# The second group's convolution inside the first group's turn, and info and mask in strips of 32 partitions

## What is computed

```
# 1. gated convolution on the group-normalised x
info = relu(info_w @ gn(x) + info_b)                 # 16 channels
mask = sigmoid(mask_w @ gn(x) + mask_b)              # 16 channels
x = x + relu(out_w @ (mask outer info) + out_b)      # 256 products -> 64 channels
# 2. linear attention on tokens t (1024 per image, one sequence per image)
t = t + attention(layernorm(t))     # q, k, v, elu+1, KV, Z, Wm, LN, W1, relu, W2, LN
# 3. mixture of 8 experts, top 2
h = layernorm(t); probs = softmax(h @ gate_w + gate_b); keep the two largest
t = t + sum over experts of weight * (gelu(h @ W1[e] + b1[e]) @ W2[e] + b2[e])
```

## Time and profile before

| | us |
|---|---|
| median of three runs | 1230.57 (1230.32 to 1233.61) |
| profiled execution, whole | 1232.37 |
| its span, first to last instruction | 1230.6 |
| PE busy | 1067.6 (87%) |
| DVE busy | 849.7 (69%) |
| ACT busy | 696.5 (57%) |
| POOL busy | 362.3 (29%) |
| mean granted TensorE clock | 0.972 of full speed |

### The profile page before, as it was taken

How to read it: one execution, slowest core, us unless ns; L and a number is a source line. 1 busy time by engine, 2 the same in 40 slices (tenths; PEclk the granted TensorE clock), 3 DMA queues, 4 the chain that set the end, 5 groups by cost and what they waited for, 6 DMA issues and landing times.

```text
span 1230.6 us, 14702 instructions
## 1 busy us (share of the span) xinstructions
PE 1067.6 (87%) x5430; PEld 502.1 (41%) x5430; DVE 849.7 (69%) x1767; ACT 696.5 (57%) x960; POOL 362.3 (29%) x276
## 2 busy tenths in 40 slices
PE   4776598989999798997989989998989979899897
PEld 2454245433454245442454433642344424444232
DVE  5665768588676976588774886859765796657543
ACT  3424365665656646656457656466565565576454
POOL 0100022234312333134231343133431233323466
PEclk8878599999999999999999999999999999999999
DMA  3110194005910086100940049200671009310480
GB/s 109 35 35 1 24 214 109 1 18 116 214 35 18 1 185 144 35 19 21 224 115 4 18 90 213 62 1 18 142 187 35 18 3 216 78 35 18 102 199 29
DMA packets 16119, 96.56 MB, mean 78 GB/s; under 512 B 3056, under 2 KB 5424, under 8 KB 11824
## 3 DMA queue, kind: packets, MB, share of 16 engines
q1 hardware_dynamic: 16048, 95.62, 33.4%
HBM read 77.79 MB, written 9.44 MB: 71 GB/s over the span
## 4 chain that ended last, share of the span: by engine, by line
PE 53%; DVE 26%; ACT 16%; issue 3%; DMA 1%; POOL 0%; DVEq 0%; POOLq 0%; SPq 0%; ACTq 0%
PE HP L691 9%; PE HP L676 9%; PE R L538 8%; PE R L486 5%; PE R L493 4%; ACT H L818 4%; PE R L504 4%; DVE SM L992 3%; PE R L615 3%; DVE T L1019 3%; PE R L552 3%; PE R L622 2%; DVE TM L1147 2%; PE R L691 2%; DVE BIG L1055 2%
## 5 line engine op out<-in xcount | busy, mean ns | idle before, releaser
L858 POOL TENSOR_TENSOR XB<-TM,XB 128x512 f32<-128x512 f32 x256 | 324.8, 1290 | 804.5 <-DVE TM L1147 804.4
L818 ACT ACTIVATE H<-HP,W 128x1024 f32<-128x1024 f32 x224 | 237.7, 1115 | 111.3 <-PE HP L676 110.1
L676 PE MATMUL HP<-XF,W1E 64*128 64x512 f32 x1024 | 255.1, 616 | 24.9 <-DVE TM L1147 24.5
L691 PE MATMUL HP<-H,W 128*64 128x512 f32 x896 | 226.5, 614 | 25.7 <-ACT H L818 25.7
L1147 DVE SCALAR_TENSOR_TENSOR TM<-HP,B2S,CWB 128x512 f32<-128x512 f32 x224 | 158.7, 741 | 119.1 <-PE HP L691 116.6
L676 PEld LDWEIGHTS HP<-XF,W1E 64*128 64x128 f32 x1024 | 87.3, 185 | 143.3 <-DVE TM L1147 82.5
L754 ACT ACTIVATE T<-R 128x512 f32<-128x512 f32 x128 | 74.0, 599 | 93.3 <-PE R L538 81.3
L691 PEld LDWEIGHTS HP<-H,W 128*64 128x64 f32 x896 | 49.9, 135 | 171.6 <-ACT H L818 119.6
L992 DVE TENSOR_REDUCE SM<-T 128x8 f32<-128x512 f32 x128 | 85.7, 684 | 41.5 <-ACT T L754 40.9
L968 DVE SCALAR_TENSOR_TENSOR BIG<-R,T 128x512 f32<-128x512 f32 x128 | 79.4, 682 | 23.6 <-PE R L486 23.6
L504 PE MATMUL R<-W,T 128*128 128x128 f32 x512 | 74.9, 294 | 15.0 <-DVE T L1011 14.0
(11 more groups left out here) (120 smaller groups left out, 1403.5 us busy)
## 6 DMA issues: line engine op xcount, KB each, us to landing
CWB<-gates_hbm SPq DMA_DIRECT2D x32, 1536.0 KB, 21.3
CWB<-gates_hbm SPq DMA_DIRECT2D x32, 512.0 KB, 9.7
X<-x SPq DMA_DIRECT2D x16, 512.0 KB, 5.9
BIG<-XN SPq DMA_DIRECT2D x32, 256.0 KB, 4.5
out<-XB SPq DMA_DIRECT2D x16, 512.0 KB, 2.7
W<-wpack SPq DMA_DIRECT2D x1, 1176.0 KB, 7.0
gates_hbm<-CWR SPq DMA_DIRECT2D x16, 64.0 KB, 1.6
W1E<-w1e SPq DMA_DIRECT2D x1, 512.0 KB, 8.4
```

Source lines behind the costliest of these rows:

```text
L676: last = mm(HP[u % BATCH][:, half(k)], W1E[img(k), e, :], XF[img(k), 1 - par, s, half(c)], start=True, stop=True)
L691: last = mm(sums_of(b, u)[img(k), :], w("w2e")[:, C * e:C * e + C], activated(b, u)[:, k, :], start=True, stop=True)
L818: f(activated(b, u).rearrange("p k t -> p (k t)"), HP[u % BATCH][:, :], ACT.Gelu, bias=col(B1E + e))\
L858: nc.gpsimd.tensor_tensor(acc, TM[:, u % BATCH, :], acc, ALU.add).then_inc(acc_done, 1)
```

## The change

1. Group 1 (EARLY) has its convolution inside turn 0. A list OPENING replaces the table for that turn; entries with `next` are stages of group 1. Its buffers are ones that nothing uses then: XF[:, 1] for the input (loaded at the start), the planes 0 to 6 of CWB for XN, T1, T2 and BIG, and HP for R. In turn 1 the convolution's stages are left out, centre_1 waits for the router's use of the R banks (cwt_done), and the input of group 2 is loaded into X in turn 1.
2. Info and mask of a slot lie in strips of 32 partitions, for the two pieces of 512 columns: info of slot s in strips 2s and 2s+1, mask in the other two; IM holds the high part and the rest behind each other in the columns. info_mask is four matmuls of 32 columns of weights into one bank, one ACT operation for info and one for mask (64 partitions), one cast and one subtraction on DVE (128 partitions). A replication is two matmuls of 32 rows that add up, for each piece. REP is loaded as eight pieces, the biases as eight small strips (BI).
3. The small statistics of the group norm have a tile of their own (SG), KVM lies in T1, and the chain's semaphore counts are kept by a running count.
4. SCHEDULE has other places for H and Y (eight batches ahead of `first_unit`, eight behind), conv_out.1 ahead of conv_out.0, `first_unit` behind centre_1.1, and finish_0 ahead of rstd_4.

The pieces stand in the order of the file: the tables, the turn, the strips and buffers, then PE's info_mask, replicate and centre_1, ACT's info_mask, DVE's info_mask. Names with a small a behind them (Xa, Ra, BIGa) are what convolution_buffers returns.

```diff
 SCHEDULE = [
-    ("channel_stats", "H"), ("gates", ""), ("gate_tokens", "Y"), ("gate_exp", ""), ("group_stats", "H"),
+    ("channel_stats", "H"), ("gates", ""), ("gate_tokens", ""), ("gate_exp", "Y"), ("group_stats", ""),
...
+EARLY = 1
+OPENING = [
...
+    "low_1.1", "high_1.0", "high_1.1", "conv_out.0", "next group_stats", "conv_out.1", "centre_1.1",
...
+            if a == 0:
+                ahead, _ = parts(EARLY, None, 1 - par)
+                for name in OPENING:
+                    first, _, rest = name.partition(" ")
+                    stage = ahead.get(rest) if rest else stages.get(name)
+                    if stage:
+                        stage()
+                return
...
+        def strip(kind, s, c):
+
+            q = 2 * (s ^ kind) + c
+            return slice(32 * q, 32 * q + 32)
...
+        def convolution_buffers(a):
+
+            if a == EARLY:
+                return XF[:, 1, :, :], CWB[:, :, 0, :], CWB[:, :, 1, :], CWB[:, :, 2, :], CWB[:, :, 3:7, :], HP
+            return X, XN, T1, T2, BIG, R
...
-                    for c in range(NCH):
-                        mm(R[s][img(c), half(c)], w("wim"), XN[:, s, half(c)], start=True, stop=True)\
-                            .then_inc(im_ps, 1)
+                    for kind in range(2):
+                        for c in range(NCH):
+                            last = mm(Ra[s][strip(kind, s, c), 0:CH], w("wim")[:, 32 * kind:32 * kind + 32], XNa[:, s, half(c)],
+                                      start=True, stop=True)
+                    last.then_inc(im_ps, 1)
...
                 def replicate(n, slots):
 
                     if n == 0 and starting(a):
                         pe.wait_ge(prep_done, 1)
                         pe.wait_ge(act_prep, 2)
-                    for s, c in pieces(slots):
+                    for s in slots:
                         if n == 0:
-                            pe.wait_ge(hl_done, nth(a + 1, s, c))
-                            if exists(a - 1):
+                            pe.wait_ge(hl_done, nth(a + 1, s))
+                            if exists(a - 1) and a != EARLY:
                                 pe.wait_ge(cwt_done, a)
                         elif n % 3 == 1:
-                            pe.wait_ge(ir_done[s], at(a * 2 + n // 3 + 1, c))
+                            pe.wait_ge(ir_done[s], at(a * 2 + n // 3 + 1, LAST))
                         else:
-                            pe.wait_ge(prod_done[s], at(a * 4 + (n + 1) // 3 + n // 3, c))
-                        mm(R[s][:, half(c)], REP[:, n, :], IM[:, s, half(c)], start=True, stop=True).then_inc(rep_ps[s], 1)
+                            pe.wait_ge(prod_done[s], at(a * 4 + (n + 1) // 3 + n // 3, LAST))
+                        for part in range(2):
+                            for c in range(NCH):
+                                rows = strip(1 if n % 3 else 0, s, c)
+                                last = mm(Ra[s][:, half(c)], REP[rows, n, :], IM[rows, s, part, :], start=(part == 0), stop=(part == 1))
+                                if part == 1:
+                                    last.then_inc(rep_ps[s], 1)
...
-                        by_token(s, c, X, w("center")).then_inc(ln_ps[s], 1)
+                        if a == EARLY:
+                            pe.wait_ge(cwt_done, a)
+                        by_token(s, c, Xa, w("center")).then_inc(ln_ps[s], 1)
...
-                    for c in range(NCH):
-                        act.wait_ge(im_ps, nth(a + 1, s, c))
-                        info, mask = slice(C * c, C * c + 32), slice(C * c + 32, C * c + 64)
-                        f(T1[0:32, s, half(c)], R[s][info, half(c)], ACT.Relu, bias=col(B_IM, info))
-                        f(T1[32:64, s, half(c)], R[s][mask, half(c)], ACT.Tanh, bias=BT[mask, :], scale=0.5)\
-                            .then_inc(im_act, 1)
+                    act.wait_ge(im_ps, nth(a + 1, s))
+                    info, mask = img(s), img(1 - s)
+                    f(T1a[info, s, 0:CH], Ra[s][info, 0:CH], ACT.Relu, bias=BI[info, 0, 0:1])
+                    f(T1a[mask, s, 0:CH], Ra[s][mask, 0:CH], ACT.Tanh, bias=BT[mask, :], scale=0.5).then_inc(im_act, 1)
...
-                    for c in range(NCH):
-                        dve.wait_ge(im_act, nth(a + 1, s, c))
-                        high = IM[0:C, s, half(c)]
-                        v.tensor_copy(high, T1[0:C, s, half(c)]).then_inc(hl_high, 1)
-                        dve.wait_ge(hl_high, nth(a + 1, s, c))
-                        v.tensor_tensor(IM[C:P, s, half(c)], T1[0:C, s, half(c)], high.bitcast(F32),
-                                        ALU.subtract).then_inc(hl_done, 1)
+                    dve.wait_ge(im_act, nth(a + 1, s))
+                    high = IM[:, s, 0, :]
+                    v.tensor_copy(high, T1a[:, s, 0:CH]).then_inc(hl_high, 1)
+                    dve.wait_ge(hl_high, nth(a + 1, s))
+                    v.tensor_tensor(IM[:, s, 1, :], T1a[:, s, 0:CH], high.bitcast(F32), ALU.subtract).then_inc(hl_done, 1)
```

117 lines of the change are left out of this document (76 added, 41 removed), and 38 rows, old and new, of tables (OPENING, SCHEDULE).

## The result

The changed kernel takes 1223.9 us (median of four runs, 1223.6 to 1224.0), the kernel before, beside it on the same chip, 1231.2. The ratio is 0.992, with a 95% interval of 0.990 to 0.995; in a second session it was 0.991 (0.989 to 0.994, 1222.8 us). The forecast was 1201 us with a range from 1184 to 1225.

A forecast was written before the change was run, and what follows sets the result against it. Full turns were taken as DVE-bound in the head, then PE-bound without a gap; turn 0 as a chain of latencies. The terms -29.9 + 3.9 + 11 - 15 = -30.0 us gave 1201 us, range 1184 to 1225.

The forecast's parts named there:

- Term 1: Head of turn 1: the second group's convolution leaves; last XF copy to centre_1 falls from 42.1 to 12.2 us, -29.9.
- Term 2: Turn 1 and tail: one batch of units moves from turn 1 into the tail, +3.9 us.
- Term 3: Turn 0: the second convolution as filling, +16 us less 2.7 and 2.3, so +11, bounds -5 and +23.
- the strips shorten the first group's own info and mask: Turn 0: ACT's eight operations of 0.68 us become four, -2.7 us.
- PE, fuller now: Turn 0: PE should be granted its full clock for more of the time (mean 0.84 before), -2.3 us.
- Term 4: Full turns: shorter info and mask work -1.5 us, replications -1.0, together -2.5 a turn, -15 for six.
- one batch's combine (two at 0.74) leaves it for the part where PE is full: Full turns: moving this combine, with the shorter info and mask work, relieves DVE's head; 1.5 us taken, bounds 0 and 4.5.
- A: Rival: the full turns don't get shorter, as DVE's saving may return as waits for GELUs; 1216 us, chance 0.20.
- C: Rival: turn 0's filling is not free and grows by +23 us, full turns stay; 1228 us, chance 0.07.
- at 146 or more C holds: Sign in turn 0: XF copies ending at 138 us fit the forecast, at 146 or more they mean C.
- B: Rival: the strips' matmuls run one after another in every group; 1251 us, slower, chance 0.11.
- D: Rival: the full turns' head gives all that DVE saves, 4.5 + 1 us a turn; 1183 us, chance 0.06.

The follow-up runs named there:

- e4: The changed kernel with eight unused 128x512 matmuls while TensorE waits for the router's choice in turn 1; 1219.7 us, ratio 0.988.
- e2: The changed kernel with the old SCHEDULE table, while turn 0 keeps OPENING; 1220.4 us, ratio 0.989.
- e11: The changed kernel run once more, unchanged, with a second profile; 1222.8 us, ratio 0.991.
- e5: The kernel before with the strips alone: no early convolution, old SCHEDULE table, in turn 0 too; 1231.9 us, ratio 0.999.
- e15: The kernel before with the strips alone, and replications waiting for each piece of 512 columns by itself; 1226.8 us, ratio 0.995.
- e3: The changed kernel without the early convolution: group 1 is convolved in turn 1, turn 0 keeps the order of OPENING; 1240.2 us, ratio 1.006.
- e13: The changed kernel with the old SCHEDULE table and replications waiting for each piece of 512 columns by itself; 1219.6 us, ratio 0.990.
- e9: The changed kernel with a replication's two loops exchanged, so two matmuls in a row use the same strip; 1223.9 us, ratio 0.993.
- e1: The kernel before with the new SCHEDULE table and nothing else; 1264.2 us, ratio 1.025.
- e7: The changed kernel with conv_out.1 of group 1 moved from the middle of centre_4 into turn 1's router wait; 1218.3 us, ratio 0.988.
- e12: The changed kernel with the old table, conv_out.1 of group 1 in turn 1's router wait and four unused matmuls behind it; 1220.8 us, ratio 0.989.
- e14: The changed kernel with the old table, info and mask in twice as many operations over half the partitions; 1241.0 us, ratio 1.006.
- e10: The changed kernel (new table) with info and mask in twice as many operations over half the partitions; 1252.5 us, ratio 1.016.

## Why the prediction was wrong, step by step

**Term 1 was right.** 11.2 us lie between XF and centre_1 (forecast 12.2), and the first gate weights are waited for by nobody. Not in the sum was that TensorE, idle for 7.56 us in the router's wait, runs centre_1 at a granted clock of 0.57 behind it: turn 1 lost 3.3 us, and e4, which fills the wait, gets 2 of them back.

**Term 2 was right in size.** +4.2 from the profile, 2.8 by e2; the forecast was 3.9. With e11's profile it would be 7.0, so one execution doesn't show it to better than 3 us.

**Term 3: the filling was near, the strips' share in it wrong.** The filling costs 11 to 13 us where +16 had been forecast for the stages. Two steps failed. The first is that "the strips shorten the first group's own info and mask", -2.7 us. In e5 turn 0 is 6.2 us longer with the strips alone: 1.1 from a start that came later, 4.0 up to centre_1 and 1.0 behind it. From group_stats to the first replication it takes 9.2 us both before and in e5, so nothing of the 2.7 arrived there. The coarser waits, which the forecast named for the full turns and booked at nothing here, are 2.7 of the 4.0 (e15 against e5); conv_out at a lower clock is 2.2 us longer in e15 too. In the order of OPENING (e3) turn 0 grows by 6.3 us, but otherwise divided: 0.5 at the start, 2.0 up to the end of centre_1 and 3.7 behind it. The cause there is open, since e13 regains nothing. The second failed step is that PE, fuller now, would be granted more of its clock, -2.3: the filled turn has 0.82 (e2, e4, e9, e11) where it had 0.84.

**Term 4: near in the sum for the strips, wrong in that the table was free.** The forecast was -2.5 us a turn, and the strips give -2.2 with the old table. They give it by another split: 2.1 from the shorter operations (forecast 1.5, half of what they save, when nearly all counts) and nothing that shows from the replications (forecast 1.0), although these do get shorter on TensorE: 7.4 to 6.1 us a turn. What failed is the step that "one batch's combine (two at 0.74) leaves it for the part where PE is full". It was named as relief for VectorE's head. But the batch's second layer goes the same way, and its 1.94 us on TensorE, in a section that has no gap, were put at nothing. Measured, the new table takes 1.5 us in the middle and gives 0.5 in the head: +0.9 a turn with the short operations. With the long ones (e1) it costs 3.4 on the mean: 2.0 in the middle of the one turn at full clock, and 3.4 to 4.9 in the others, with a lower clock behind the wait that the second layer left. Two turns of the kernel after have such a stretch of 3.4 us at half clock, and add 1.6 each; before, six turns were only 0.35 above six times 145.0. So -2.2 + 0.9 = -1.3 a turn, -7.8 for six, +3.3 and -0.35: the measured -4.8.

**The rivals.** No rival named the table. A (the turns don't get shorter, 1216) is half true: 1.3 us a turn, or 0.8 with the disturbed turns, is between none and 2.5. C (filling at its upper bound, turn 0 +23) was nearest in size, 1228 for 1223.9; turn 0 got to 19.6, but only 12 of it is filling. The test that I had set, "at 146 or more C holds", would have misled: the number was reached in part by another cause. That the measured time lies inside the range is no merit of the working: terms 3 and 4 missed by 8.6 and 10.2 us, and another 3.3 were in no term. B is refuted: the strips overlap. Four matmuls on a slot's two strips last 0.73 us and eight on all four strips 0.74, where one by itself lasts 0.49 in the median. The Trainium skill (TensorE: Matmul & The Clock Gate, Part 3) has distinct row groups start within some 4 ns of each other. The trace agrees for fp32r within its scatter: in the block at 575.23 the four matmuls on four strips start 3, 10 and 3 ns apart, and the other four 0.33 us later. D is refuted: the head does give all that VectorE saves, but that is 2.0 to 2.6 us and not 4.5.

## What to carry to other kernels

When a change brings a new order together with a new layout, price each alone: here the order costs 2.5% by itself, and with the layout's shorter operations 0.9 us a turn. When a step moves to another stretch, move its work on every engine with it: the combine that left VectorE's head took a second layer into the stretch in which TensorE has no gap, and there it cost 1.5 us, or 2.0 in e1. Cut a period at its stages before naming the stage that a change costs. A coarser wait cost nothing that shows in the full turns (142.8 us either way) and 2.7 us in turn 0, so look it up in the thinnest stretch of the program too. And before a few us of one trace are explained, read a second execution of the same kernel: here the same turn 0 ended up to 4.6 us apart.

## Unexpected of the hardware

The granted clock in a thin stretch. Identical instructions of turn 0 ended between 144.2 and 146.5 us in four executions (e2, e4, e11, after), and at 142.6 and 147.2 in e7 and e12, with the half-clock stretches in different places. Unused matmuls put into waits restored the clock just behind them (centre_1 6.43 to 3.81 us, the first blocks 2.1 to 0.75), but in turn 0 the mean over 100 us rose from 0.83 to 0.85 only. In the full turns the middle's clock goes with the wait before the first replication: with 0.7 us (before, e14) it is 1.00 in all five turns, with 1.45 (after) it is 0.94 in two of five, with 2.7 to 2.8 (e1, e10) it is 0.89 to 0.94 in nine of ten.

VectorE's cast on 128 partitions takes 1.06 us and not 0.43, and the difference 1.64 and not 0.69, where an operation of POOL runs beside them. These are of one full turn of the kernel after, the undisturbed pair, POOL's row and the pair beside it:

```profile
554.75 0.43 DVE L1032 CAST IM<-T 128x512 fp32r<-128x512 f32 x1
555.21 0.69 DVE L1034 TENSOR_TENSOR IM<-T,IM 128x512 fp32r<-128x512 f32 x1
...
563.69 2.68 POOL L930 TENSOR_TENSOR XB<-TM,XB 128x512 f32<-128x512 f32 x2 [4.36 <-DVE TM L1224]
...
564.19 1.06 DVE L1032 CAST IM<-T 128x512 fp32r<-128x512 f32 x1
565.28 1.64 DVE L1034 TENSOR_TENSOR IM<-T,IM 128x512 fp32r<-128x512 f32 x1
```

It holds for the whole trace: of this kernel's 32 such operations the 13 that overlap with one of POOL last 1.06 to 1.67 us, and the 19 that don't last 0.41 to 0.43 (cast) and 0.69 (difference). The kernel before has the same, 1.05 and 1.64 us for six pairs. So of the two pairs in a full turn one costs twice and more what the other does.
